# Layer 0 of a graph network kernel: a new column order of the gathered rows, one product for two harmonics, one sum of four parts

## The reference, cut to what matters

```python
xs_e, xv_e = xs[src], xv[src]                  # rows of the sources
es, ev = edge_feat[:, 0], edge_feat[:, 1:4]    # 4 harmonics of an edge
out_s = (einsum('eu,uo->eo', xs_e * es[:, None], W_ss) / sqrt(64)
         + einsum('eud,ed,uo->eo', xv_e, ev, W_vv) * ISQ3 / sqrt(32)) * ISQ2
out_v = (einsum('eu,ed,uv->evd', xs_e, ev, W_sv) * ISQ3 / sqrt(64)
         + einsum('eud,e,uv->evd', xv_e, es, W_vs) * ISQ3 / sqrt(32)) * ISQ2
messages = concatenate([out_s, out_v.reshape(-1, 96)], axis=1)
messages = messages * sigmoid(edge_scalars @ W_rad.T + b_rad)
agg = segment_sum(messages, dst, num_segments=n)
```

## Time and profile before

| what | value |
|---|---|
| median of 3 runs | 4367.61 us (4367.43 to 4368.17) |
| the profiled execution's own time | 4365.39 us |
| its span, first to last instruction | 4363.6 us |
| mean granted TensorE clock | 0.789 |
| busy: TensorE, VectorE | 3885.0 us, 3885.0 us (89% each) |
| busy: GpSimd, ScalarE | 3137.4 us (72%), 2657.9 us (61%) |
| bytes read from HBM | 618.56 MB |

### The profile page before, as it was taken

How to read it: one execution, slowest core, us unless ns; L and a number is a source line. 1 busy time by engine, 2 the same in 40 slices (tenths; PEclk the granted TensorE clock), 3 DMA queues, 4 the chain that set the end, 5 groups by cost and what they waited for, 6 DMA issues and landing times.

```text
span 4363.6 us, 64697 instructions
## 1 busy us (share of the span) xinstructions
PE 3885.0 (89%) x14024; PEld 2504.5 (57%) x14025; DVE 3885.0 (89%) x8520; ACT 2657.9 (61%) x8218; POOL 3137.4 (72%) x3268
## 2 busy tenths in 40 slices
PE   7898999989999898899878898899888888889887
PEld 5565666656666666666655555555555555555556
DVE  4999999999999999999768898988888998898997
ACT  5666666666666666666555566666656666666664
POOL 4777777777777777777457777777777777777771
PEclk7656555565555556655799999999999999999999
DMA  9666666666666666666333333333333333333332
GB/s 291 192 194 192 191 193 192 192 193 193 190 193 192 192 194 191 190 194 192 113 99 102 102 100 102 104 103 102 103 99 101 103 103 103 104 102 103 104 104 60
DMA packets 245760, 640.04 MB, mean 147 GB/s; under 512 B 57101, under 2 KB 95439, under 8 KB 245627
## 3 DMA queue, kind: packets, MB, share of 16 engines
q0 software_dynamic: 181136, 556.56, 46.5%
q1 hardware_dynamic: 64592, 83.11, 6.1%
HBM read 618.56 MB, written 20.88 MB: 147 GB/s over the span
## 4 chain that ended last, share of the span: by engine, by line
DVE 52%; PE 16%; issue 15%; DVEq 6%; DMA 4%; ACT 3%; POOL 2%; SPq 0%; POOLq 0%; ACTq 0%
PE ps L1005 11%; DVE work L702 10%; DVE onehot L746 10%; DVE work L676 7%; DVE arena L754 4%; DVE work L726 3%; DVE work L669 3%; DMA arena<-table,srcs 3%; DVE work L723 2%; DVE work L689 2%; DVEq L811 2%; DVE acc L754 2%; ACT work L487 2%; PE ps L982 2%; POOL arena L390 2%
## 5 line engine op out<-in xcount | busy, mean ns | idle before, releaser
L390 POOL DMA_INDIRECT arena<-table,srcs x1596 | 1544.0, 967 | 486.2 <-issue 432.9
L390 POOL DMA_INDIRECT work<-table,srcs x1596 | 1523.0, 954 | 500.4 <-issue 482.7
L1005 PE MATMUL ps<-work,onehot 128*128 128x384 f32 x3608 | 1311.6, 510 | 224.6 <-DVE work L733 130.3
L487 ACT ACTIVATE work<-arena,harm 128x160 f32<-128x160 f32 (+1 forms) x3224 | 985.4, 388 | 452.6 <-DMA arena<-table,srcs 435.6
L1005 PE MATMUL ps<-arena,onehot 128*128 128x161 f32 x3608 | 1020.4, 459 | 198.9 <-DVE arena L712 167.4
L1005 PEld LDWEIGHTS ps<-arena,onehot 128*128 128x128 f32 x3608 | 872.8, 305 | 513.8 <-issue 440.6
L487 ACT ACTIVATE work<-work,harm 128x96 f32<-128x96 f32 (+1 forms) x3224 | 1071.4, 415 | 121.4 <-DMA work<-table,srcs 63.1
L1005 PEld LDWEIGHTS ps<-work,onehot 128*128 128x128 f32 x3608 | 671.1, 195 | 775.2 <-issue 328.4
L982 PE MATMUL ps<-wrad,escal 49*128 49x320 f32 x1612 | 890.1, 697 | 0.0
L746 DVE SCALAR_TENSOR_TENSOR onehot<-ps,bases,dst_sh 128x512 f32<-128x512 f32 x902 | 670.8, 744 | 14.6 <-DVE acc L754 7.3
L702 DVE TENSOR_REDUCE work<-work 128x256 f32<-128x768 f32 (+1 forms) x806 | 654.1, 851 | 0.7 <-ACT ps L515 0.4
(11 more groups left out here) (131 smaller groups left out, 2222.4 us busy)
## 6 DMA issues: line engine op xcount, KB each, us to landing
escal<-in_escal SPq DMA_DIRECT2D x404, 98.0 KB
arena<-table,srcs POOLq DMA_INDIRECT x1596, 3.5
work<-table,srcs POOLq DMA_INDIRECT x1596
table<-work SPq DMA_DIRECT2D x49, 224.0 KB, 6.1
dst_sh<-in_dst_sh SPq DMA_DIRECT2D x52, 160.0 KB, 3.2
table<-work SPq DMA_DIRECT2D x7, 784.0 KB, 4.0
acc<-in_xd SPq DMA_DIRECT2D x1, 3920.0 KB, 22.4
arena<-in_xd SPq DMA_DIRECT2D x7, 560.0 KB, 4.3
```

Source lines behind the costliest of these rows:

```text
L390: pool.indirect_dma_start(out=rows[:, j, t, :], out_offset=None, in_=table, in_offset=bass.IndirectOffsetOnAxis(ap=of[:, j, t:t + 1], axis ...
L487: last = nc.scalar.activation(u[:, t, to:to + c1 - c0], r[:, t, c0:c1], ACT.Copy, scale=harm[:, j, at:at + 1])
L1005: last = mm(bank(to)[:, 0:(MSG0, MSG1)[l]], onehot[:, b, t, :], m[:, j % 2, t, :], start=t == 0, stop=t == TPS - 1)
```

## The change: what it does

- The columns of the table are laid out anew: 0 to 191 for the second and third harmonic (96 each), 192 to 287 for the first, 288 to 447 for the fourth. The weights and the rows of `xT` are placed to suit on the host; the table keeps its 448 columns, and TensorE, the copies and the gathers keep their sizes. One scaling of weights on ScalarE goes (5 become 4 in all).
- VectorE copies the harmonics of a round (64 numbers a partition) into PSUM (`harm0`, in bank 7, which layer 0 doesn't use otherwise), once a round, with a wait for itself. The copy ScalarE stages in `harm` stays, for ScalarE.
- VectorE's product with the second harmonic and the four additions with the third are replaced by one product for both, 768 numbers a partition, with the harmonics from PSUM. It waits for the gathers instead of ScalarE's first four (`s_whead` is gone), and frees the rows for GpSimd when it is done. The wait for `s_agg` stands behind it, the one for `s_add` is gone.
- The weighted rows have 672 columns instead of 544. One sum over four parts 128 columns apart gives the 64 scalars, behind a wait for ScalarE's second four; one addition, in place and with both inputs in SBUF, completes the 96 vector columns (384 numbers a partition), behind the wait for the sigmoid. The product with the radial factors is as before.
- ScalarE's eight instructions keep their sizes and their order (160 columns, then 96), and read and write other columns.

```diff
+        harm0 = hps[:, 0:4 * TPS * SLOTS].rearrange("p (j c) -> p j c", j=SLOTS)
...
-                weight(u, r, 3, 96, 256, 128, j % PAIR).then_inc(s_whead, 1)
-                weight(u, r, 0, 256, 352, 288).then_inc(s_wtd[0], 1)
+                weight(u, r, 3, 288, 448, 64, j % PAIR)
+                weight(u, r, 0, 192, 288, 256).then_inc(s_wtd[0], 1)
...
                 if l == 0:
-                    dve.wait_ge(s_whead, s + 1)
+                    if j == 0:
+                        nc.vector.tensor_copy(harm0, of_round(i, slice(0, SLOTS), slice(TPS, 5 * TPS)).bitcast(f32)).then_inc(s_harmp[0], 1)
+                        dve.wait_ge(s_harmp[0], i + 1)
+                    dve.wait_ge(s_rows[0][j], (i + 1) * 16 * TPS)
                     u, r = weighted0[:, j % DEEP0, :, :], rows0[:, j, :, :]
-                    nc.vector.tensor_tensor(u[:, :, 384:480], r[:, :, 352:448], by(1), ALU.mult)
-                    for t in range(TPS):
-                        if t == 1:
-                            dve.wait_ge(s_add[0], s + 1)
-                        if t == TPS - 1 and not opens:
-                            dve.wait_ge(s_agg[0], s + 1)
-                        to = u[:, t, 128:224]
-                        last = nc.vector.scalar_tensor_tensor(to, r[:, t, 0:96], harm[:, j, 4 * t + 2:4 * t + 3], to,
-                                                              ALU.mult, ALU.add)
-                    last.then_inc(s_wone[0], 1)
+                    nc.vector.tensor_tensor(u[:, :, 384:640].rearrange("p t (k c) -> p t k c", k=2)[:, :, :, 0:96],
+                                            r[:, :, 0:192].rearrange("p t (k c) -> p t k c", k=2),
+                                            bc(harm0[:, j, :].rearrange("p (t k) -> p t k", k=4)[:, :, 1:3], 3, [P, TPS, 2, 96]),
+                                            ALU.mult).then_inc(s_wone[0], 1)
+                    if not opens:
+                        dve.wait_ge(s_agg[0], s + 1)
...
-                summed(u[:, :, 0:MS], 160, 3)
+                dve.wait_ge(s_wtd[0], s + 1)
+                parts = u[:, :, 160:672].rearrange("p t (k c) -> p t k c", k=4)
+                nc.vector.tensor_reduce(u[:, :, 0:MS], parts[:, :, :, 0:MS].rearrange("p t k c -> p t c k"), AX.X, ALU.add)
                 dve.wait_ge(s_act[0], s + 1)
-                summed(u[:, :, MS:2 * MS], 224, 2).then_inc(s_part[0], 1)
+                vectors = u[:, :, MS:DIM].rearrange("p t (k c) -> p t k c", k=3)
+                nc.vector.tensor_tensor(vectors, vectors, u[:, :, 256:640].rearrange("p t (k c) -> p t k c", k=3)[:, :, :, 0:MV],
+                                        ALU.add).then_inc(s_part[0], 1)
                 dve.wait_ge(s_part[0], s + 1)
```

More of the change, by code:

```diff
@@ L45 @@
 WEIGHTED = 640
-PARTS0 = 544
+PARTS0 = 672
 TAIL1 = P + ROW1 - MV
@@ L204, in mk_gnn_resnorm_d2_gnn_r8_694f30_kernel @@
         s_harmp = [sem(f"harmonics_in_psum{l}") for l in range(2)]
-        s_whead = sem("scalar_parts_weighted")
         s_wone = [sem(f"rows_weighted_by_dve{l}") for l in range(2)]
@@ L228, in mk_gnn_resnorm_d2_gnn_r8_694f30_kernel @@
         I8, I32, I96 = MS ** -0.5, MV ** -0.5, (MS + MV) ** -0.5
-        SCALED0 = [(w0a[0:64, 128:192], I8 * ISQ2), (w0a[0:64, 0:128], I8 * ISQ3 * ISQ2), (w0a[0:64, 192:448], I8 * ISQ3 * ISQ2),
+        SCALED0 = [(w0a[0:64, 384:448], I8 * ISQ2), (w0a[0:64, 0:384], I8 * ISQ3 * ISQ2),
                    (w0a[64:128, :], I32 * ISQ3 * ISQ2), (w0b[:], I32 * ISQ3 * ISQ2)]
@@ L445, in _ @@
             act.wait_ge(s_w0, 32)
-            for w, c in SCALED0[:3]:
+            for w, c in SCALED0[:2]:
                 nc.scalar.activation(w, w, ACT.Copy, scale=c).then_inc(s_w0scaled, 1)
@@ L624, in _ @@
                     dve.wait_ge(s_w0, 32)
-                    for w, c in SCALED0[3:]:
+                    for w, c in SCALED0[2:]:
                         nc.vector.tensor_scalar(w, w, c, None, ALU.mult).then_inc(s_w0scaled, 1)
@@ L697, in messages0 @@
                 dve.wait_ge(s_wone[0], s + 1)
-                def summed(to, at, k):
-                    parts = u[:, :, at:at + k * P].rearrange("p t (k c) -> p t k c", k=k)
-                    return nc.vector.tensor_reduce(to, parts[:, :, :, 0:MS].rearrange("p t k c -> p t c k"), AX.X, ALU.add)
                 def by_half(x):
                     return x.rearrange("p (h k) c -> p h k c", h=2)
-                summed(u[:, :, 0:MS], 160, 3)
+                dve.wait_ge(s_wtd[0], s + 1)
+                parts = u[:, :, 160:672].rearrange("p t (k c) -> p t k c", k=4)
+                nc.vector.tensor_reduce(u[:, :, 0:MS], parts[:, :, :, 0:MS].rearrange("p t k c -> p t c k"), AX.X, ALU.add)
                 dve.wait_ge(s_act[0], s + 1)
-                summed(u[:, :, MS:2 * MS], 224, 2).then_inc(s_part[0], 1)
+                vectors = u[:, :, MS:DIM].rearrange("p t (k c) -> p t k c", k=3)
+                nc.vector.tensor_tensor(vectors, vectors, u[:, :, 256:640].rearrange("p t (k c) -> p t k c", k=3)[:, :, :, 0:MV],
+                                        ALU.add).then_inc(s_part[0], 1)
                 dve.wait_ge(s_part[0], s + 1)
@@ L971, in _ @@
                 mm(p[:, 0:ROW0], x0[:, of_tile], w0a[:], start=True, stop=False)
-                mm(p[:, 32:128], x1[:, of_tile], w0b[:], start=False, stop=True).then_inc(s_tmm, 1)
+                mm(p[:, 224:320], x1[:, of_tile], w0b[:], start=False, stop=True).then_inc(s_tmm, 1)
             pe.wait_ge(s_tev, NODE_TILES)
@@ L1206 @@
     by_component = np.concatenate([s_of, *v_of])
+    v_of_kept = [MS + MV * d + np.arange(MV) for d in range(3)]
     xd = placed(NODES_PAD, DIM, (0, 0, x[:, by_component]))
@@ L1230 @@
     ins = {
-        "xT": xd.T, "xd": xd,
+        "xT": xd.T[np.concatenate([s_of, *(v_of_kept[d] for d in (1, 2, 0))])], "xd": xd,
         "srcs": np.concatenate([by_supertile(src, 0).transpose(1, 0, 2), np.zeros((P, SLOTS, TPS), src.dtype)], axis=1),
@@ L1237 @@
         "attr": placed(NODES_PAD, 1, (0, 0, attr)).reshape(NODE_TILES, P).T,
-        "w0a": placed(P, ROW0, (0, 0, wsv), (0, 128, wss), (64, 192, wvs), (96, 224, wvs),
-                      (64, 256, wvv), (0, 320, wsv), (0, 352, wsv), (96, 384, wvv)),
+        "w0a": placed(P, ROW0, (0, 0, wsv), (64, 32, wvv), (0, 96, wsv), (96, 128, wvv), (0, 192, wsv),
+                      (64, 320, wvs), (96, 352, wvs), (0, 384, wss)),
         "w0b": placed(P, 96, (0, 0, wvv), (0, 64, wvs)),
```

2 lines of the change are left out of this document (removed).

## The result

The changed kernel takes 4475.95 us (median of 4 runs, 4471.27 to 4482.05) against 4367.89 us: ratio 1.0243, 95% interval 1.0231 to 1.0255. It is slower by 2.4%, where 0.3% less was forecast. The profiled execution took 4474.24 us, its span is 4472.4 us, 108.8 us longer than that of before.

The account below looks back on a forecast made before the run. GpSimd's gathers, 5.00 us a supertile plus a surplus, were taken as the bound, VectorE just keeping up. From 4365.4 us, −13 (gathers) and −1 (layer's end) gave 4351.4, or 4353.6 as median of runs; range 4335 to 4374.

Parts of the forecast that it names:

- the sum of four parts: VectorE in layer 0: one sum reading 1024 numbers at 1.33 ns each, 1.36 us a supertile.
- I cost it at nothing but the end of the layer: VectorE's 0.30 us less a supertile, 121 us over 403, gains nothing within layer 0, as GpSimd's 5.00 us cover it.
- The slower rival: Layer 0: the new addition locks onto a gather's start, 41 us more surplus, time 4408; chance 0.1.
- The gathers' part: Layer 0: gather surplus of 35 us from operations with two SBUF inputs falls to 22, gain 13, bounds 35 and −41.
- Product, addition, copy, ScalarE and the landings: Layer 0: product 0.950 us, addition 0.553, copy 0.22 once a round; ScalarE's sizes unchanged, no new stall for landing rows.
- The layer's end: From layer 0's last gather start to its last addition, 15.84 us before: 1 us less, bounds 0 and 2.
- Layer 1: Untouched, but starting some 14 us earlier against dips of TensorE's clock: costed at 0, bounds ±8 us.
- Rival 1: Layer 0: all of the gathers' surplus goes, down to GpSimd's floor, −35 −2, time 4331; chance 0.1.
- Rivals 2 to 4: Layer 0 gathers: addition locks onto starts (4408, chance 0.1); nothing changes (4366.6, 0.27); PSUM product stretches them (within that 0.27).

Follow-up runs that it names:

- The forms: Sums, copies and additions of varied part counts and distances, run alone at the changed kernel's end: four parts 128 columns apart about 1.9 us, three 1.03.
- three-part run: Changed kernel with its sum over only the first three of four parts, the last left out: 4337.97 us against 4360.71 for the kernel before.

## Why the prediction was wrong

**The step that failed** is "the sum of four parts reads 1024 numbers: both old forms give 1.33 ns a number read, so 1.36 us". It measured 1.904 us. Two points had been taken for a line through the origin: 681 ns for 512 numbers and 1021 for 768. The forms show 0.69, 1.03, 1.91 and 2.31 us for two to five parts, so there was a step just outside what the trace of before held. No range stood on this term; it should have had one, since no row showed four parts.

**The sum with this term put right**: VectorE has not 0.30 us less a supertile but 3.50 − 3.26 = 0.24 more. Times 403 that is 97 us, of the 109 by which the last gather is later; VectorE's busy time on the page, which counts overlapping instructions once, has grown by 110.

**"I cost it at nothing but the end of the layer, since GpSimd's 5.00 us cover it"** held for less work and was never worked out for more. The prediction said itself that VectorE "has little slack", but it added up only what the change takes and gives, never VectorE's whole cycle, and so had no price for an excess. There was hardly any cover: with a copy and its wait once a round the kernel before already loses 0.6% (the run with its harmonics in PSUM), though its gathers got shorter. VectorE's 188 to 189 of 200 us and its 32.5 us of waiting for ScalarE said so. The slower rival was looked for in the placing of one addition, not in a longer VectorE operation, the nearest way to lose 2%.

**The gathers' part held.** By the table the layer's surplus comes from operations with both inputs in SBUF, and the prediction's shares of it, 19 us for the product and 16 for the four additions, are close to the 21.1 and 13.9 of the table. It expected 22 us to stay beside the new addition; in the run with the sum of three in PSUM, where that addition is the one operation left with two SBUF inputs, it is 20.3, and the last gather starts at 2094.0 us where 2096 were forecast. In the changed kernel itself the addition catches only 36 gathers, for 6 us: the gathers' mean of 952 ns is partly luck of where the late VectorE puts the addition. The three-part run, which has the change's structure and a cheap sum, is some 20 us faster than before, where the forecast had 14 for a sum of 1.36 us. The rule of the Trainium skill (SBUF — State Buffer, "Who interferes with whom") by which a tensor_tensor leaves descriptor generation alone is an inference there, and the pair with the sum in SBUF and in PSUM, 13 us apart, goes against it. The same section also says that a VectorE instruction with two SBUF inputs contends with a GpSimd instruction that reads SBUF. The gathers read their row numbers there, and the table agrees with that rule, which the prediction did not weigh.

**Product, addition, copy, ScalarE and the landings** came as forecast: 949 against 950 ns, 542 against 553, 228 against 220, and the product waited for rows only at the start of the layer (9.4 us, once). **The layer's end** was forecast 1 us shorter and came 7.4 us longer in the changed kernel, because VectorE still had a backlog; in the three-part run it is 1.0 us shorter. **Layer 1** takes 2015 us from first to last gather instead of 2022, within the 8 us allowed.

**Rival 1** (the floor of the gathers, 4331, 37 us under before) is not reached by any version: the best ends 24 us under the kernel before on its chip, with 20 us of surplus left. **Rivals 2 to 4** were not what happened: the gathers' surplus fell, and those that start within the product with an operand in PSUM are not lengthened (265 of them in the changed kernel, mean 948 ns). None of the four was a longer sum.

## What to carry to other kernels

Price an operation by a row of its own access pattern, and where none exists take a range as wide as a doubling: two rows of shorter forms are no line. Where two engines' cycles are nearly equal, what a change adds to one counts almost in full and what it removes counts hardly at all; add up the whole cycle of the engine that is changed, and don't only look at whether the other one waits. Here a sum of four far-apart parts was better cut into three and one, with the intermediate in PSUM, than written as one instruction. And beside an engine that issues gathers back to back, put one input of a two-input VectorE operation in PSUM, if that costs VectorE no extra work; with a copy more it was slower here.

## What the runs showed of the hardware

- VectorE reads four or more fp32 numbers of SBUF that lie 4 columns (16 bytes) or more apart, innermost, at a surplus: sums of four 1.87 to 1.95 us for 1024 numbers, against 1.22 for numbers 1 or 2 columns apart; five far apart 2.31 (1280 numbers), eight 3.59 (2048), against 2.29 for eight adjacent. Three far apart pay little (1.03 us for 768, adjacent 0.95). A copy of the same 1024 numbers takes 1.17 us against 0.69 along the columns, and from PSUM four far apart are cheaper than from SBUF (0.42 us for 256 numbers against 0.59).
- A gather issued by GpSimd that starts within a VectorE operation with both inputs in SBUF is held to about its end (longest 1322 ns beside a median of 946 in the kernel before, 1469 beside 949 with an addition of 512 numbers); one with one input in PSUM, and a sum with its single input in SBUF, leave it at the median. For one addition of 256 numbers that came to 13 us of the kernel's time.
